# Moving the PSUM copies of the per-tile projections from VectorE to ScalarE

## The reference

```
disp = ln(x) @ W_disp        # 16 heads x 16 values per token
val  = ln(x) @ W_val         # 16 heads x 64 values
strain[t, j] = disp[t-63+j] - disp[t]                 # j = 0..63
bond   = gelu(strain @ W_strain + rel_emb @ W_pos) @ W_bond
damage = sigmoid(gelu(strain @ W_dmg + b_dmg) @ W_dmg_out + b_dmg_out)
w = softmax_j(bond - 10 * damage)
x = x + (sum_j w[j] * val[t-63+j]) @ W_cproj
x = x + feed_forward(ln(x))
```

## Time and profile before

| | |
|---|---|
| median of 3 runs | 3396.5 us (3394.89 to 3396.85) |
| profiled execution, slowest core | 3396.09 us, of which the span 3394.6 us |
| spans of the 8 cores | 3387.5 to 3394.6 us |
| busy, share of the span | PE 50%, PEld 14%, DVE 29%, ACT 27% |
| mean granted TensorE clock | 0.578 on the slowest core |
| copies on DVE (L272, L288, L307, L321, L324) | 17 + 34 + 34 + 34 + 34 |

### The profile page before, as it was taken

One profiled execution on the slowest core, in us unless ns is written; L12 is line 12 of the kernel. 1 busy time (PEld: TensorE's weight loads), 2 busy tenths in 40 slices (PEclk: granted clock), 3 DMA queues, 4 the chain that ended last, 5 costly groups with the idle time before them and its releaser, 6 DMA issues.

```text
span 3394.6 us, 22054 instructions; the slowest of 8 cores (3387.5 to 3394.6 us)
## 1 busy us (share of the span) xinstructions
PE 1701.9 (50%) x4568; PEld 469.6 (14%) x4568; DVE 968.1 (29%) x2737; ACT 931.1 (27%) x1253; POOL 17.3 (1%) x32
## 2 busy tenths in 40 slices
PE   0055445435444445445555445554554374747777
PEld 0011111111111111111111112221121010101111
DVE  0013333353324333452232332122212504132001
ACT  0004445344543554642243232131000010101010
POOL 0000000000000000000000000000000000000000
PEclk9998565556565555655555555555555555555555
DMA  8400000010000100021110011111111101001001
GB/s 128 98 22 10 19 10 10 3 19 10 19 10 4 19 10 13 1 50 37 41 31 25 25 38 32 37 31 44 47 44 31 31 7 54 20 13 50 25 25 44
DMA packets 134680, 100.45 MB, mean 30 GB/s; under 512 B 111120, under 2 KB 112288, under 8 KB 134560
## 3 DMA queue, kind: packets, MB, share of 16 engines
q1 hardware_dynamic: 125152, 78.88, 8.7%
q0 software_dynamic: 9408, 20.15, 3.1%
HBM read 74.86 MB, written 35.40 MB: 32 GB/s over the span
## 4 chain that ended last, share of the span: by engine, by line
PE 40%; issue 20%; ACT 20%; DVE 15%; DMA 5%; DVEq 1%; ACTq 0%; SPq 0%; POOLq 0%
ACT s_actT L438 10%; ACT s_actT L428 6%; PE ps L676 5%; PE ps L842 5%; PE ps L814 5%; PE ps L788 5%; PE ps L283 4%; DMA Ebuf<-s_zero 4%; PE ps L451 3%; DVE s_eh L492 2%; DVE s_argT L417 2%; PE ps L302 2%; PE ps L612 2%; PE ps L608 2%; PE ps L634 2%
## 5 line engine op out<-in xcount | busy, mean ns | idle before, releaser
L451 PE MATMUL ps<-s_actT,s_bd 128*32 128x512 bf16 (+1 forms) x1280 | 461.2, 509 | 621.0 <-ACT s_actT L438 445.4
L438 ACT ACTIVATE s_actT<-s_argT,s_pcols 128x512 bf16<-128x512 bf16 (+1 forms) x640 | 368.3, 646 | 25.1 <-DVE s_argT L417 13.1
L428 ACT ACTIVATE s_actT<-s_argT,s_bdmgc 128x2048 bf16<-128x2048 bf16 x128 | 256.2, 2002 | 191.4 <-DVE s_argT L417 181.0
L438 ACT ACT_TABLE_LOAD x36 | 46.2, 1283 | 858.8 <-DVE s_argT L417 858.7
L451 PEld LDWEIGHTS ps<-s_actT,s_bd 128*32 128x32 bf16 x1280 | 126.2, 120 | 940.0 <-issue 926.0
L417 DVE TENSOR_TENSOR s_argT<-s_dD 128x512 bf16<-128x512 bf16 (+1 forms) x640 | 203.6, 381 | 78.3 <-ACT s_actT L438 60.1
L417 DVE TENSOR_TENSOR s_argT<-s_dS 128x512 bf16<-128x512 bf16 (+1 forms) x640 | 203.5, 381 | 62.2 <-ACT s_actT L438 47.6
L676 PE MATMUL ps<-s_wcp,s_atok 128*128 128x512 bf16 x272 | 158.9, 584 | 57.5 <-DVE s_atok L654 19.5
L842 PE MATMUL ps<-s_wval,s_kact 128*128 128x512 bf16 x256 | 149.5, 584 | 60.3 <-DVE s_x2r L851 23.9
L788 PE MATMUL ps<-s_xk,s_wkT 128*128 128x512 bf16 x256 | 149.5, 584 | 58.0 <-DVE s_xk L774 19.9
L283 PE MATMUL ps<-s_wval,s_lnfm 128*128 128x512 bf16 x272 | 145.6, 535 | 47.0 <-DVE s_lnfm L272 7.3
(11 more groups left out here) (104 smaller groups left out, 1254.0 us busy)
## 6 DMA issues: line engine op xcount, KB each, us to landing
s_wbt<-Ebuf SPq DMA_DIRECT2D x68, 191.0 KB, 3.3
Ebuf<-s_zero SPq DMA_DIRECT2D x16, 544.0 KB
X2buf<-s_xrel SPq DMA_DIRECT2D x17, 512.0 KB, 2.6
s_x<-X2buf POOLq DMA_DIRECT2D x17, 512.0 KB, 4.0
s_xt<-xs SPq DMA_DIRECT2D x33, 256.0 KB, 3.9
s_xrel<-xs SPq DMA_DIRECT2D x33, 256.0 KB, 4.1
s_x2r<-X2buf SPq DMA_DIRECT2D x16, 512.0 KB, 3.7
out<-s_x2r SPq DMA_DIRECT2D x16, 512.0 KB, 2.6
```

Of the source, the lines that this page charges most:

```text
L428: P.emit("scalar", (lambda half=half: (lambda e: e.activation(out=s_actT[:, 2048 * half:2048 * half + 2048], in_=s_argT[:, 2048 * half:204 ...
L438: P.emit("scalar", (lambda slot=slot, W=W, bias=bias: (lambda e: e.activation(out=s_act[slot][:, 0:W], in_=s_arg[slot][:, 0:W], func=AF.Ge ...
L451: (lambda e: e.matmul(PS[bank][32 * q:32 * q + 32, 0:W], s_bd32[:, pi * 128 + v * 32: pi * 128 + v * 32 + 32], s_act[slot][:, 0:W], start= ...
```

## The change

All 153 copies from PSUM in `part_te`, `part_val`, `part_disp` and `part_dsd` go from VectorE's `tensor_copy` to ScalarE's `activation` with the function Copy. The semaphore by which others learn of them changes from `sv` to `ss`. In `part_disp` and `part_dsd` two waits of TensorE also become narrower: where the matmuls waited for everything emitted on VectorE so far (`P.now("sv")`), they wait for the last copy of the same part, kept in `ev_prev`, and, for the first half, for older copies only.

```
     def part_te(b):
-        wtp = {"sv": max(ln_done[b], lnfm_evac.get(b - 2, 0), val_evac.get(b - 1, 0)),
+        wtp = {"sv": ln_done[b], "ss": max(lnfm_evac.get(b - 2, 0), val_evac.get(b - 1, 0)),
...
-        P.emit("vector", (lambda b=b, bank=bank: (lambda e: e.tensor_copy(
-            s_lnfm[:, b * 1024:(b + 1) * 1024], PSB[bank][:, 0:1024])))(),
-            waits={"st": P.now("st")}, inc="sv")
-        lnfm_evac[b] = P.now("sv")
+        P.emit("scalar", (lambda b=b, bank=bank: (lambda e: e.activation(
+            out=s_lnfm[:, b * 1024:(b + 1) * 1024], in_=PSB[bank][:, 0:1024], func=AF.Copy)))(),
+            waits={"st": P.now("st")}, inc="ss")
+        lnfm_evac[b] = P.now("ss")
...
     def part_disp(b):
+        ev_prev = [0]
         for m in range(2):
             bank = 2
-            wvv = merge_w({"sv": max(lnfm_evac[b], dSD_evac.get(b - 1, 0), P.now("sv"))}, ld_w["W_disp"])
+            wvv = merge_w({"ss": max(lnfm_evac[b], dSD_evac.get(b - 1, 0), ev_prev[0])},
+                          ld_w["W_disp"])
...
+            ev_prev[0] = P.now("ss")
...
     def part_dsd(b):
+        ev_prev = [0]
         for m in range(2):
...
-                waits={"sv": max(sv_dscr[b], P.now("sv"))}, inc="st")
+                waits={"ss": max(sv_dscr[b], ev_prev[0])}, inc="st")
...
                     if jgl == 0 and pi == 0 and k == 0:
-                        wv["sv"] = dSD_evac[min(tb_hi, NTB - 1)]
+                        wv["ss"] = max(wv.get("ss", 0), dSD_evac[min(tb_hi, NTB - 1)])
```

More of the change, by code:

```diff
@@ L279, in part_val @@
             bank = eh
-            wvv = merge_w({"sv": max(lnfm_evac[b], val_evac.get(b - 2, 0)),
+            wvv = merge_w({"ss": max(lnfm_evac[b], val_evac.get(b - 2, 0)),
                            "dV": vspill.get(b - 2, 0)}, ld_w["W_val"])
@@ L287, in part_val @@
                     waits=wvv if cb == 0 else None, inc="st")
[L288 to L291, removed]
+            P.emit("scalar", (lambda b=b, eh=eh, bank=bank: (lambda e: e.activation(
+                out=s_vstage[b % 2][:, eh * 512: eh * 512 + 512], in_=PS[bank][:, :], func=AF.Copy)))(),
+                waits={"st": P.now("st")}, inc="ss")
+        val_evac[b] = P.now("ss")
         P.emit("sync", (lambda b=b: (lambda e: e.dma_start(
             out=d_val.ap()[128 * b:128 * b + 128, :], in_=s_vstage[b % 2][:, :])))(),
-            waits={"sv": val_evac[b]}, inc="dV", amt=16)
+            waits={"ss": val_evac[b]}, inc="dV", amt=16)
         vspill[b] = P.now("dV")
     def part_disp(b):
+        ev_prev = [0]
         for m in range(2):
             bank = 2
-            wvv = merge_w({"sv": max(lnfm_evac[b], dSD_evac.get(b - 1, 0), P.now("sv"))}, ld_w["W_disp"])
+            wvv = merge_w({"ss": max(lnfm_evac[b], dSD_evac.get(b - 1, 0), ev_prev[0])},
+                          ld_w["W_disp"])
             for cb in range(8):
@@ L306, in part_disp @@
                     waits=wvv if cb == 0 else None, inc="st")
[L307 to L310, removed]
+            P.emit("scalar", (lambda m=m, bank=bank: (lambda e: e.activation(
+                out=s_dscr[:, m * 128:m * 128 + 128], in_=PS[bank][:, 0:128], func=AF.Copy)))(),
+                waits={"st": P.now("st")}, inc="ss")
+            ev_prev[0] = P.now("ss")
+        sv_dscr[b] = P.now("ss")
     def part_dsd(b):
+        ev_prev = [0]
         for m in range(2):
@@ L320, in part_dsd @@
             st_d = P.now("st")
[L321 to L327, removed]
+            P.emit("scalar", (lambda b=b, m=m: (lambda e: e.activation(
+                out=s_dS[:, m * COLS + 128 * b: m * COLS + 128 * b + 128], in_=PS[3][:, 0:128], func=AF.Copy)))(),
+                waits={"st": st_d}, inc="ss")
+            P.emit("scalar", (lambda b=b, m=m: (lambda e: e.activation(
+                out=s_dD[:, m * COLS + 128 * b: m * COLS + 128 * b + 128], in_=PS[2][:, 0:128], func=AF.Copy)))(),
+                inc="ss")
+            ev_prev[0] = P.now("ss")
+        dSD_evac[b] = P.now("ss")
     TPARTS = (part_ln, part_te, part_val, part_disp, part_dsd)
```

## The result

The changed kernel took **3331.7 us** (median of 8 runs, 3330.7 to 3333.2) against 3396.3 us for the kernel before, timed beside it (8 runs, 3394.9 to 3397.6): a ratio of 0.981, with a 95% interval of 0.980 to 0.982. That is 64.6 us less, where 61.7 had been worked out.

What follows compares the result with a forecast made beforehand. Waits between engines were taken to bound the kernel, not any engine's load. Prologue 8.6, parts between paths 30.1, pairs 20.5 and ends 2.5 sum to 61.7 us off 3396.1: forecast 3334 us, range 3312 to 3356.

Steps and rivals of the forecast that it cites:

- Prologue: 150 to 283 us, where TensorE sets the pace: disp and dsd matmuls start earlier through narrower waits; 8.6 us won.
- Parts between paths: 25 parts in the chunks, each between two Gelu paths, 6 layer norm ones untouched; the other 19 win 30.1 us.
- the lead: VectorE makes subtractions beside TensorE's matmuls, so Gelu follows the copy by 0.09 us instead of 1.74; 1.65 us per part.
- Pairs around a combination: 34 parts, 17 pairs around Tanh, VectorE's operation and Exp, with Tanh now behind the copy ahead; 20.5 us won.
- te–val: Three pairs around a combination; TensorE's val part hides the combination; 1.4 us won each, 4.2 together.
- val–disp: Four pairs around a combination; disp's first half no longer waits for VectorE's operation; 2.1 us three times, 4.7 in chunk 0.
- disp–dsd: Four pairs around a combination; copies stand behind Exp; -0.3 us twice and +2.3 twice, together 4.0 won.
- Chunk ends: Six parts at the ends of chunks: chunk 0's gain some 2.8 us, chunk 1's lose 0.3; 2.5 won.
- Prices of the copies: Copies from PSUM on ScalarE: 1.02, 0.60 and 0.28 us for 1024, 512 and 128 columns.
- The slower rival: Parts between Gelus: Copy needs another table, so 36 parts pay 72 loads, 92 us; kernel at 3426 us; chance 3%.
- The clock: TensorE's granted clock shifts with the denser work: about 3305 us if faster (12%), 3350 us if slower (9%).
- No lead: Subtractions behind parts still wait for ScalarE's copies, so only 17 us are won; 3379 us; chance 4%.

Runs made afterwards that it cites:

- the third experiment: The changed kernel, but the first subtractions behind each te, val, disp or dsd part also wait for ScalarE's copies of that part; 3387.7 us.
- the last kernel: Against the kernel before: copies on VectorE, narrow waits, three groups of subtractions ahead of parts (two at layer norm) and attention tiles, combination ahead of the part; 3025.9 us.
- the second experiment: The changed kernel with TensorE's broad waits on VectorE put back in the disp and dsd parts, copies staying on ScalarE; 3353.4 us.

## Why the prediction was right

Point by point, against the chain of Gelu starts before and after:

- **Prologue**, 8.6 predicted. 7.5 by the trace; the first tile load landed 1.6 us later in the profiled execution after (158.73 against 157.13), so 9.1 by the kernel. Sqrt of the layer norm, the copies and TensorE's second pair stand as worked out: TensorE's val matmuls start at 197.26, 2.16 us behind Sqrt's start at 195.10, where it had been 4.43:

```profile
195.10 0.29 ACT L204 ACTIVATE s_lncol<-s_lncol,s_cst 128x1 f32<-128x1 f32 x1 [1.01 <-DVE s_lncol L203]
195.53 0.28 ACT L325 ACTIVATE s_dS<-ps 128x128 bf16<-128x128 f32 x1
```

- **Parts between paths**, 30.1 predicted, 31.5 measured: te 6.6 and 6.6, val 7.0 and 6.8, disp and dsd 16.5 and 17.9 (1.73 to 1.81 for most instead of 1.65; 1.66 is the lead and 0.12 is the copy's engine, by the third experiment), layer norm 0 and 0.1.
- **Pairs around a combination**, 20.5 predicted, 23.4 measured: te–val 4.2 and 6.0, layer norm–te 3.9 and 4.4, val–disp 11.0 and 11.2, disp–dsd 4.0 and 3.9, dsd–layer norm -2.6 and -2.1. te–val's surplus is one pair with 3.06 where the two others have 1.47; in that pair the granted clock was 0.51 before and 0.66 after, so the two traces don't compare there. disp–dsd came out by some luck: 2.9, 2.4, -1.3 and -0.1 for the 2.3 twice and -0.3 twice of the prediction.
- **Chunk ends**, 2.5 and 2.4.
- **Prices of the copies**: right to 3 ns per copy, no table load. The slower rival, a load at each Copy, is dead: the counts of loads are those of before.
- **The clock**: 0.581 after, 0.578 before on the profiled cores, 0.582 and 0.581 over all eight, so that rival took nothing either way.
- **No lead**, the rival put at 3379, was made real by the third experiment and took 3387.7. Its price had been too low: the 14 pairs lose 1.66 each too, 23 us and not 15.

The chain won 64.7 us by chunk 2's next to last path, and 63.1 by the last Gelu; the spans differ by 62.2, and the medians by 64.6. These are two cores, 7 and 1, whose clock stretches fall differently, and spans of one execution's cores differ by 9 us; where the 2.5 us between 64.7 and 62.2 went is not shown. Against 61.7 the terms as measured (9.1, 31.5, 23.4 and 2.4) add up to 66.4. None of the four is off by more than 2.9 us, and three were put too low, so the sum isn't right by terms that cancel.

One argument fell, though no number hung on it. The prediction held a rule against the change (the Trainium skill, "ScalarE: Activation LUTs", "Rules for kernel authors": simple elementwise work belongs on VectorE) and priced it by copy time alone, 3 us. Copy time is indeed that little. But with the subs issued ahead, copies on VectorE are 99 us better, since ScalarE can then run on. So the rule's advice holds in this kernel once the order is right, for a reason that the page doesn't give. Of the change's gain the narrow waits need no move of the copies at all, and the lead can be had by the order alone; the move itself costs some 15 us.

## What to carry to other kernels

When an in-order engine waits for a producer at one instruction, look at what stands behind it in the stream and needs nothing new, and issue that first; moving the waiting instruction to another engine only moves the place where nothing can run ahead. Ask which engine's next work can be done during the wait, and keep the copy off that one. Waits that name "everything so far" of a busy engine are worth narrowing by themselves (23.8 us here), and the two edits all but add up.

## What the hardware showed that was not expected

- **TensorE's granted clock changed with the order of the work, and not in step with the gaps closed.** Every trace has two levels, 1.2 and 2.4 GHz. From the mean clock and the span, the time at 2.4 GHz was 550 us before and 545 after; 530 and 513 us in the kernels with two groups ahead (wide and narrow waits), although these are 171 and 189 us faster than before; and 569, 623 and 654 us with three groups, with the combination first and in the last kernel (means over eight cores; mean clock 0.58 in the first four, then 0.59, 0.60, 0.61). The Gelu paths' matmuls of 512 columns follow it: 556 and 554 ns, then 562 and 568, then 544, 524 and 509. So in the last three kernels TensorE's own work shrank as well, but closing gaps alone didn't do it, or the kernels with two groups would show it too. What decides it, and how much of the time it is, isn't shown.
- **The first tile load lands at another time on each core and in each execution**: on the profiled cores at 157.1 us before, 158.7 after, 161.5 in the second experiment and 156.7 in the last kernel; and within the one execution of the kernel before, the first layer norm, which waits for it, starts between 151.7 and 159.3 us on the eight cores. The prologue hangs on it, so its terms can't be read from two traces to better than some us unless the landing is taken off, as above.
